# Two selections of operands moved to VectorE's bank pairs, a new order for the middle stage, and added products that nobody reads

## The reference, cut to what matters

```python
x = x + attn(layernorm(x))            # 16 heads of 8, relative positions clipped at 64
x = x + xattn(ctx, layernorm(x))      # shifts rows, a strided convolution of 32 context rows
x = x + ffn(layernorm(x))             # a second attention (rotary, 16 heads of 8) and experts
# attn, for each head
score = q @ k.T + einsum('qd,qkd->qk', q, pe_k);  p = softmax(score)
ctx = p @ v + einsum('qk,qkd->qd', p, pe_v)
# ffn
q, k = rope(x @ Wq), rope(x @ Wk_c @ Wk);  sa = softmax(q @ k.T / sqrt(8)) @ v
x = rmsnorm(x + sa @ Wo);  out = rmsnorm(x + shared(x) + two chosen experts of eight)
```

## Time and profile before

| | us |
|---|---|
| median of 3 runs | 489.73 |
| lowest and highest | 483.55, 494.31 |
| the profiled execution, its own time | 492.59 |
| its span in the profile | 490.7 |

### The profile page before, as it was taken

The page is one execution under the profiler, slowest core; times in us unless marked ns, Lnnn a source line. Parts: engine busy times, 40 slices in busy tenths (PEclk is TensorE's granted clock), DMA queues, the critical chain, the costliest instruction groups (busy, mean ns, idle before and its releaser), DMA issues.

```text
span 490.7 us, 14472 instructions
## 1 busy us (share of the span) xinstructions
PE 386.2 (79%) x6093; PEld 228.2 (47%) x6093; DVE 268.8 (55%) x481; ACT 250.3 (51%) x520; POOL 175.0 (36%) x358
## 2 busy tenths in 40 slices
PE   1769888888898887596788887877868877986974
PEld 0313445656676665354335554543325555443431
DVE  4647553665777774467019877511386580143555
ACT  1445564765676663338554656564525677621300
POOL 6420153464666756624145121340001420002463
PEclk9955555988999997889558989875565799998999
DMA  7200000000000000000000400000000000000000
...
DMA packets 12078, 8.19 MB, mean 17 GB/s; under 512 B 4558, under 2 KB 11102, under 8 KB 11886
## 3 DMA queue, kind: packets, MB, share of 16 engines
...
...
## 4 chain that ended last, share of the span: by engine, by line
PE 62%; ACT 13%; DVE 11%; POOL 6%; issue 6%; DMA 1%; SPq 0%; ACTq 0%; POOLq 0%; DVEq 0%
PE ps L1032 15%; PE ps L1010 7%; ACT arena L636 7%; PE ps L996 6%; PE ps L966 5%; DVE m_qk L777 4%; PE ps L1120 4%; PE ps L1050 4%; PE ps L942 4%; PE ps L1151 4%; PE ps L1137 3%; PE ps L1105 2%; ACT eb L623 2%; PE ps L1056 1%; POOL rstd L398 1%
## 5 line engine op out<-in xcount | busy, mean ns | idle before, releaser
L777 DVE TENSOR_REDUCE m_qk<-ps 128x2 f32<-128x1024 f32 x128 | 153.4, 1221 | 104.3 <-PE ps L966 104.2
L636 ACT ACTIVATE arena<-ps 128x512 f32<-128x512 f32 x256 | 139.2, 597 | 68.0 <-PE ps L1010 66.3
L1032 PE MATMUL ps<-arena,v_sb 128*20 128x128 f32 x2048 | 82.4, 310 | 1.6 <-ACT ctx L645 1.6
L1010 PE MATMUL ps<-q_op,k_op 62*128 62x128 bf16 (+1 forms) x1024 | 57.0, 236 | 25.8 <-ACT arena L636 21.1
L561 POOL TENSOR_TENSOR arena<-arena,eb 128x256 f32<-128x256 f32 x64 | 47.2, 737 | 79.9 <-ACT eb L623 40.6
L1032 PEld LDWEIGHTS ps<-arena,v_sb 128*20 128x20 f32 x2048 | 57.9, 111 | 17.2 <-issue 6.5
L1010 PEld LDWEIGHTS ps<-q_op,k_op 62*128 62x128 bf16 (+1 forms) x1024 | 39.9, 103 | 54.9 <-ACT arena L636 34.4
L966 PE MATMUL ps<-k_op,q_op 48*128 48x512 bf16 x256 | 59.5, 465 | 6.7 <-DVE m_qk L777 6.0
L623 ACT ACTIVATE eb<-ps 128x512 f32<-128x512 f32 (+1 forms) x64 | 31.3, 541 | 34.9 <-PE ps L996 32.2
L397 POOL TENSOR_SCALAR var<-mv 128x4 f32<-128x4 f32 (+1 forms) x16 | 3.2, 201 | 116.8 <-ACT eb L707 55.8
L562 POOL TENSOR_TENSOR arena<-arena,eb 128x192 f32<-128x192 f32 x64 | 39.1, 611 | 0.0
...
## 6 DMA issues: line engine op xcount, KB each, us to landing
...
q_op<-farT SPq DMA_DIRECT2D x32, 3.0 KB
q_op<-farT SPq DMA_DIRECT2D x32, 1.5 KB
...
```

What stands on the lines that cost most here:

```text
L636: act.activation(p_ring[:, k % SLOTS_P, e, :], ps[:, bank, :], ACT.Exp).then_inc(sm["bank_free"], 1)
L777: dve.tensor_reduce(m_qk[:, u % NT, n:H:PAIRS], ps[:, banks, :], AX_X, ALU.max).then_inc(sm["pair_free"], 1)
L1010: i = pe.matmul(ps[:, into[e], jt * P:jt * P + P], k_op[64 * e:64 * e + kr, n, b * S + jt * P:b * S + jt * P + P], q_op[64 * e:64 * e + kr ...
L1032: i = pe.matmul(out, v_sb[:, IT * b + jt, 4 * n + hh, :], rhs, start=(n == 0 and jt == 0), stop=(u >= NT and jt == IT - 1), skip_group_che ...
```

## The change

- Both kinds of turn leave the ring and go into VectorE's bank pairs. ScalarE copies the first head pair out and counts `picked`; VectorE copies the second and counts `pair_free`. Only in turns 2 to 7 of the first sequence does ScalarE copy both (`act_alone`). PE waits for both counts before it uses the pair of banks again (`before`, `came`). The `again` turns come in the order of `TURNS`.
- The ring is banks 4, 5 and 6 from the start, and `QK_BANKS` moves.
- `busy(bank, n)` makes n products of 128 rows and 512 columns (bf16) into a bank that the next real product overwrites: one behind each of the first eight transposes, six ahead of the first turn, one ahead of each of the 32 turns, 46 in all. Ahead of the first transposes stand 12 products of the identity with itself, and the transposes now wait for `sel` as well.
- Middle stage: the root is a step of its own (`root`), earlier in GpSimd's queue; the eight normalizations of the first half are VectorE's; the split of k in the second half is VectorE's; all steps from `norm` on are half a step to one and a half later, and the `again` turns stand 0.7 apart, not 1.
- Units 8 to 15, the front of the end and the end are 2 to 4.5 steps later in the list, the third expert step of the first half stands ahead of the second half's `xT`.

```diff
...
 GROUP = 12
-QK_BANKS = ((2, 3), (7, 0))
+QK_BANKS = ((2, 6), (7, 5))
...
-AGAIN_AT = (103, 112, 121, 130, 148, 156, 164, 172)
-FRONT_AT = (157, 199.5)
-LAST = 191.6
+AGAIN_AT = (105, 115, 125, 134, 150, 158, 166, 174)
+FRONT_AT = (161.5, 201.5)
+LAST = 193.6
+TURNS = ((0, 0), (0, 1), (1, 0), (0, 2), (1, 1), (0, 3), (1, 2), (1, 3))
...
     for b, t in enumerate(MID_AT):
-        plan += [(t, 5, "y", b, 0), (t + 1, 1.5, "stat", b, 0), (t + 2, 1.5, "aggr", b, 0),
-                 (t + 4, 4, "norm", b, 2), (t + 6, 4, "mem", b, 0), (t + 7, 4, "conv", b, 0), (t + 8, 4, "shifted", b, 0),
-                 (t + 9, 1.5, "stat", b, 1), (t + 10, 1.5, "aggr", b, 1), (t + 12, 4, "norm", b, 3),
-                 (t + 13.5, 4, "xT", b, 0), (t + 15, 4, "proj", b, 0), (t + 16, 4, "proj", b, 1), (t + 16.5, 4, "v2", b, 0),
-                 (t + 17, 4, "split", b, 0), (t + 18, 4, "split", b, 1)]
-        plan += [(t + 20 + k, 4, "again", b, k) for k in range(8)]
+        plan += [(t, 5, "y", b, 0), (t + 1, 1.5, "stat", b, 0), (t + 2, 1.5, "aggr", b, 0), (t + 2.2, 1.5, "root", b, 0),
+                 (t + 4.5, 4, "norm", b, 2), (t + 6.5, 4, "mem", b, 0), (t + 7.7, 4, "conv", b, 0), (t + 8.5, 4, "shifted", b, 0),
+                 (t + 9.5, 1.5, "stat", b, 1), (t + 10.5, 1.5, "aggr", b, 1), (t + 10.7, 1.5, "root", b, 1), (t + 13, 4, "norm", b, 3),
+                 (t + 15, 4, "xT", b, 0), (t + 16.5, 4, "proj", b, 0), (t + 17.5, 4, "proj", b, 1), (t + 18.5, 4, "v2", b, 0),
+                 (t + 18, 4, "split", b, 0), (t + 19.2, 4, "split", b, 1)]
+        plan += [(t + 21.5 + 0.7 * k, 4, "again", b, k) for k in range(8)]
...
-    plan += [(162.5, 5, "gate", 0, 0), (165, 5, "group_exp", 0, 0), (170, 5, "expert_exp", 0, 0)]
+    plan += [(167, 5, "gate", 0, 0), (169, 5, "group_exp", 0, 0), (173, 5, "expert_exp", 0, 0)]
...
-    plan += [(t + d, 5, "expert", 0, n) for n, d in enumerate((7, 9, 16, 17))]
...
     plan += [(t + 12 + n, 5, "mlp", 1, n) for n in range(4)]
-    plan += [(t + 12.5, 5, "gate", 1, 0), (t + 15.5, 5, "group_exp", 1, 0), (t + 16.5, 5, "expert_exp", 1, 0), (t + 18, 5, "shared", 1, 0)]
+    plan += [(t + 11.9, 5, "gate", 1, 0), (t + 15.5, 5, "group_exp", 1, 0), (t + 16.2, 5, "expert_exp", 1, 0), (t + 18, 5, "shared", 1, 0)]
...
-    of_act = {"relk": 1, "pick": 2, "rel_rows": 1, "far_rows": 1, "qk_rows": 1, "bias": 2, "scores": 2, "back": 1,
-              "w_cT": 1, "w_full": 1, "mem": 1, "xT": 1, "v2": 1, "again": 2, "gate": 1}
+    of_act = {"relk": 1, "rel_rows": 1, "far_rows": 1, "qk_rows": 1, "bias": 2, "scores": 2, "back": 1,
+              "w_cT": 1, "w_full": 1, "mem": 1, "xT": 1, "v2": 1, "gate": 1}
...
             for _ in range(of_act[kind]):
-                if (kind == "pick" and u == 0) or kind == "relk":
-                    bank = 4 + len(uses) % 4
-                else:
-                    bank = min((4, 5, 6), key=lambda b: last.get(b, -1))
+                bank = min((4, 5, 6), key=lambda b: last.get(b, -1))
                 uses.append((bank, last.get(bank)))
                 last[bank] = len(uses) - 1
-        if kind in ("rel", "max", "fin", "y", "conv", "proj", "y2", "mlp", "shared", "expert"):
+        if kind in ("pick", "again", "rel", "max", "fin", "y", "conv", "proj", "y2", "mlp", "shared", "expert"):
             pair[(kind, u, n)] = len(pair)
...
-            return k % 2, PICK_ORDER[k // 2]
+            return TURNS[k][0], PICK_ORDER[TURNS[k][1]]
...
+            of_k, two = picks_of(n) if kind == "pick" else again_of(n)
+            return of_k, [(k_op if of_k else q_op)[:, p, u * S:u * S + S] for p in two]
+
+        def act_alone(kind, u, n):
+            return kind == "pick" and u == 0 and n >= 2
...
-                if kind == "norm" and p >= 2:
-                    pool.wait_ge(sm["aggr2_done"], 2 * u + p - 1)
-                    root(1.0, LN_EPS, tiles_of(u), 1, None)
+                if kind == "root":
+                    pool.wait_ge(sm["aggr2_done"], 2 * u + p + 1)
+                    root(1.0, LN_EPS, tiles_of(u), 1, "root_done")
+                if kind == "norm" and p >= 2 and u == 1:
+                    pool.wait_ge(sm["root_done"], 2 * u + p - 1)
                     if p == 3:
                         pool.wait_ge(sm["shift_in"], 96 * (u + 1))
                     for tt in range(IT * u, IT * u + IT):
                         pool.tensor_scalar(xn[:, tt, :], x[:, tt, :], mv[:, tt, 0:1], rstd[:, tt:tt + 1],
                                            ALU.subtract, ALU.mult).then_inc(sm[("ln2_out", "ln3_out")[p - 2]], 1)
-                if kind == "split" and u == 1:
+                if kind == "split" and u == 1 and p == 0:
...
+                if kind in ("pick", "again"):
+                    of_k, both = filled(kind, u, n)
+                    k = pair[(kind, u, n)]
+                    act.wait_ge(sm["pair_full"], k + 1)
+                    for e, into in enumerate(both if act_alone(kind, u, n) else both[:1]):
+                        got = ps[:, PAIR_BANKS[k % 2].start + e, :]
...
+                    i.then_inc(sm["picked"], 1)
...
-                if kind == "again":
-                    of_k, two = again_of(n)
-                    for k, p in enumerate(two):
-                        bank = emptied(kind, u, n, k)
-                        if of_k:
-                            act.activation(k_op[:, p, u * S:u * S + S], ps[:, bank, :], ACT.Identity, bias=cols[:, C_ONE_QK:C_ONE_QK + 1]
-                                           ).then_inc(sm["bank_free"], 1)
-                        else:
-                            act.activation(q_op[:, p, u * S:u * S + S], ps[:, bank, :], ACT.Identity).then_inc(sm["bank_free"], 1)
...
+                if kind in ("pick", "again"):
+                    of_k, (_, into) = filled(kind, u, n)
+                    got = ps[:, banks.start + 1, :]
+                    if act_alone(kind, u, n):
+                        dve.wait_ge(sm["pair_free"], k)
+                        dve.sem_inc(sm["pair_free"], 1)
+                    elif of_k:
+                        dve.tensor_scalar(into, got, cols[:, C_ONE_QK:C_ONE_QK + 1], None, ALU.add).then_inc(sm["pair_free"], 1)
+                    elif kind == "pick":
+                        into, same = by_groups(into)
+                        dve.tensor_copy(into, same(got)).then_inc(sm["pair_free"], 1)
+                    else:
+                        dve.tensor_copy(into, got).then_inc(sm["pair_free"], 1)
+                if kind == "norm" and n >= 2 and u == 0:
+                    dve.wait_ge(sm["root_done"], n - 1)
+                    if n == 3:
+                        dve.wait_ge(sm["shift_in"], 96)
+                    for tt in range(IT * u, IT * u + IT):
+                        dve.tensor_scalar(xn[:, tt, :], x[:, tt, :], mv[:, tt, 0:1], rstd[:, tt:tt + 1],
+                                          ALU.subtract, ALU.mult).then_inc(sm[("ln2_out", "ln3_out")[n - 2]], 1)
...
-                if kind == "split" and u == 0:
+                if kind == "split" and (u == 0 or n == 1):
                     other_parts(dve, link, n, u)
...
+            def busy(bank, n):
+
+                for _ in range(n):
+                    pe.matmul(ps[:, bank, :], sel[:, 0, 0, :], sel[:, 0:2, :, :].rearrange("p n a r -> p (n a r)"), start=True, stop=True)
+
             pe.wait_ge(sm["ld_id"], 16)
+            for _ in range(12):
+                pe.matmul(ps[:, 2, 0:P], ident[:, :], ident[:, :], start=True, stop=True)
+            pe.wait_ge(sm["ld_sel"], 16)
             for b in range(B):
                 for tt in range(IT * b, IT * b + IT):
                     pe.wait_ge(sm["ln_out"], tt + 1)
                     pe.transpose(ps[:, b, (tt % IT) * P:(tt % IT) * P + P], xn[:, tt, :], ident[:, :]).then_inc(sm["xT_psum"], 1)
+                    busy(2, 1)
...
+            before = sorted(pair, key=pair.get)
+
+            def came(turn):
+                pe.wait_ge(sm["pair_free"], pair[turn] + 1)
+                pe.wait_ge(sm["picked"], turns.index(turn) + 1)
...
                         pe.wait_ge(sm["pair_free"], k - 1)
+                        if before[k - 2][0] in ("pick", "again"):
+                            pe.wait_ge(sm["picked"], turns.index(before[k - 2]) + 1)
+                    else:
+                        pe.wait_ge(sm[("split_done", "vf_ready")[k]], 1)
...
+                if kind in ("pick", "again"):
+                    of_k, two = picks_of(n) if kind == "pick" else again_of(n)
+                    if kind == "pick":
+                        if u == 0 and n == 0:
+                            busy(banks.start, 6)
+                        pe.wait_ge(sm["split_done"], 2 * u + of_k + 1)
+                    else:
+                        pe.wait_ge(sm["k_split" if of_k else "q_split"], u + 1)
+                    busy(banks.start, 1)
                     for part in range(3):
-                        for bank, p in zip(into, two):
```

(6 more changed lines are left out.)

64 lines of the change are left out of this document (23 added, 41 removed).

## The result

The changed kernel takes 455.8 us (median of four runs, 453.8 to 461.6), beside 490.1 for the kernel before on the same chip: ratio 0.933, interval 0.920 to 0.945. Six more runs on another chip gave 458.4 us, 0.934 (0.930 to 0.939). Medians take in every run, while ratios and their intervals leave out runs more than 1.5% above the fastest of their kernel. The profiled execution took 453.8 us with a span of 451.7 (before: 492.6 and 490.7).

A forecast was written before the change was run, and what follows sets the result against it. PE was taken to set the pace, through its clock and gaps. Terms 0 + 4.6 + 1.7 - 1 - 8.7 - 9 - 1 - 3 = -16.4 us gave 476.2 from the profiled 492.6, or 473 us against the median; range 459 to 490.

The forecast's parts named there:

- Start and turns 2 to 7: Kernel start: turn 2 begins where it did before, net 0; then turns 3.4 us apart at the low clock, +4.6 us.
- The next eight turns: Turns after turn 7: added products cost 3.4 us, half given back by split copies and freer ring, +1.7 us.
- 86 to 170 us: Where PE streams units at clock 0.96: single clock dips, one just behind a turn, -1 us.
- Middle stage, first half: Gaps ahead of `mem` and `xT` gone, -2.1 and -5.1; clock -3, normalizations on VectorE +1.5; sum -8.7 us.
- The two stretches of second-attention turns: `again` turns in both halves: less idle, added products and higher clock together -4.5 us each, -9 us.
- The idle term: Each second-attention stretch: of 7.2 us PE idle, 4.5 us goes as VectorE takes one copy per turn.
- The clock term: Each second-attention stretch: low clock costs 6 to 7 us; about half the stretch at full clock, -2.5 us.
- rival 1: First turns: the clock stays up, period 2.5 us, the rest of the stretch faster too; 461 us, chance 0.10.
- Rival 2: Both later stretches: clock unchanged and added products fully paid; 480 to 482 us, chance 0.20.
- Rival 3: Middle stage: gaps only move to `proj` or the first `again` turn, +7; 480 to 483 us, chance 0.12.
- Rival 4: Bank pairs serialize, turns wait for VectorE, period over 4 us, products cost 14.4 us; 501 us, chance 0.12.
- The end: Second half's transposes: an `expert` step of 3.5 us fills the 3.20 us gap ahead of them, -3 us.

The follow-up runs named there:

- the banks alone: Kernel before with turns in VectorE's two bank pairs, ScalarE making both copies except turns 0 and 1, old times, no added products: 471.8 us, 0.961.
- ScalarE's copies alone: Changed kernel with both copies of every turn but the first two on ScalarE: 463.0 us, 0.946.
- the new times alone: Kernel before with the new step times and new order of turns, turns still in the ring, no added products: 490.3 us, 0.994.
- corner products: Changed kernel with each added 512-column product cut to 32 rows and 32 columns of the array, identity products kept: 466.7 us, 0.951.

## Why the prediction was right or wrong

**Start and turns 2 to 7.** Right in the period at the low clock (3.39 us from turn 4 on; the clock fell at 26.5 us, so turn 3 still came 2.4 us behind turn 2) and near in the products (0.52 and 0.32 us for 0.45 and 0.25). Wrong in "net 0" for turn 2: it came 2.4 us earlier. I took the casts at their old length, and they fell from 3.13 to 0.75 us, as they now came ahead of GpSimd's addition. My working had nothing on that order; here it was luck. From turn 2 to turn 7 it is 15.8 us for 11.7, +4.1 where I had +4.6. The next eight turns cost nothing up to the first `pv`, where I had +1.7. From turn 7 to there it takes 33.7 us in both kernels, 31.4 without products, 32.0 with the banks alone and 34.7 with ScalarE's copies alone. So the products cost 2.4 us and not 3.4, and banks and copies gave all of it back.

**86 to 170 us.** Sign right, -5.0 instead of -1. PE is busy 2.7 us less, as the clock came up at 81 us and not 86 and the dips behind went, and idle 2.4 us less (10.0 for 12.4); I had put nothing for the idle time. The banks alone have that too (9.7).

**Middle stage, first half.** Right: -7.5 for -8.7, both gaps gone. One size was wrong: I held the normalizations at 3.7 us on VectorE, and four took 1.81 and 1.85. I had carried over the total of four. Each is held only until the GpSimd instruction beside it ends: at the start those took 0.60 to 1.15 us one behind the other, here 0.73 and 0.59, and two of each four met none. GpSimd was not idle beside the 1.11 us either, as I wrote: its root of 128x4 numbers ran there for 1.0 us and held nothing up. The Trainium skill, "GPSIMD Engine Reference", section 8, says that the two engines share their interfaces to SBUF and contend. The trace agrees (0.34 us alone, 0.62 to 0.78 beside a multiplication).

**The two stretches of second-attention turns: the step that failed.** "-4.5 idle, +2.5 products, -2.5 clock", -9 us for both; with the units up to their first `pv` they gave -24.6. (The 5.0 between them come from the tables of times: fewer steps stand there, 606 recorded products for 661, and the new times alone make it 43.3 us for 48.9.) The idle term was too small: nearly all of the 7 us went, as two-bank steps no longer share three banks. The clock term was wrong in kind. I expected the full clock over half of a stretch, helped by added whole-array products. It held over all of both, and the banks alone do most of that, with no added product (0.60 to 0.90, 0.56 to 0.83; 5.0 and 5.4 us less of busy time), while the products in the old structure lift nothing. Up to the first `pv` the banks alone give -12.6 and -8.2 us, where the whole change has -11.6 and -13.0; the second stretch needs VectorE's copies too (41.3 us without them, 36.4 with). A gap costs twice there: its own length, and the low clock that goes with such a stretch; I had read the second price from the rows (6 to 7 us a stretch) and then took a third of it.

**Rivals.** The clock did stay up, but not where rival 1 had it: in the first stretch it is 0.60, and turns 4 to 7 are at the low level. Rival 2 (the clock unchanged later) was given 0.20 and is what the old structure does with the products. Rival 3 fell: no gap moved to `proj` (0.83 us ahead of its second part) or to turn 16. Rival 4 fell by its own sign: a period of 3.39 us, under 4. Its other half, the price of the products, was real: 46 recorded, 18.6 us of PE, and the kernel with fewer of them is 5 us ahead by turn 15.

**The end.** Wrong: the expert step stands ahead of the transposes as forecast, but the wait of 3 us went behind them, to ScalarE's copy of them. So PE's idle time fell by 0.9 us only, and 2.9 us of busy time at the lower clock (0.91 for 0.96) turned -3 into +2.

The Trainium skill, "TensorE: Matmul & The Clock Gate", table "Why this matters for your kernels", asks to keep TensorE busy and to avoid long idle gaps. The banks alone agree with that (idle 6.9 to 0.5 us, clock 0.60 to 0.90), though no single wait in the old stretches was over 1.1 us. The corner products do not: as busy as with whole ones, 97% from 305.6 to 323 us, and still at 0.73.
